# Two graph-attention layers on one core: layer-1 mask rows made by ScalarE inside the layer-0 attention, and layer-0 projection software-pipelined

## What is computed

```python
# layer 0, 8 heads of 64
data = (h @ W.T + b).reshape(N, 8, 64)
e = leaky_relu(src.T[:, :, None] + trg.T[:, None, :], 0.01) + adj     # src, trg: one number per node and head
x = x + softmax(e) @ data
# layer 1, 8 heads of 64, on h = relu(layernorm(x)) again
a = maximum(adj, eye)
atts = q @ k.T / 8 - 1e16 * (1 - a)
x = x + softmax(atts) @ v @ Wo
```

## Time and profile before

| | us |
|---|---|
| median of the runs | 4757.16 |
| the profiled execution | 4749.95 |
| its span | 4748.2 |
| PE busy in the span | 4406.2 (93%) |
| DVE busy | 3713.2 (78%) |
| POOL busy | 3452.3 (73%) |
| ACT busy | 3083.7 (65%) |
| layer-0 projection, first to last operation | 0 to 207 |
| layer-0 attention | 210 to 1688 |
| layer-1 projection | 1692 to 2017 |
| layer-1 attention | 2021 to 4748 |

### The profile page before, as it was taken

The page is one execution under the profiler, slowest core; times in us unless marked ns, Lnnn a source line. Parts: engine busy times, 40 slices in busy tenths (PEclk is TensorE's granted clock), DMA queues, the critical chain, the costliest instruction groups (busy, mean ns, idle before and its releaser), DMA issues. The chain is left out here.

```text
span 4748.2 us, 116365 instructions
## 1 busy us (share of the span) xinstructions
PE 4406.2 (93%) x42765; PEld 2133.6 (45%) x43276; DVE 3713.2 (78%) x7749; ACT 3083.7 (65%) x5769; POOL 3452.3 (73%) x2969
## 2 busy tenths in 40 slices
PE   6699999999999969859999999999999999999998
PEld 3222222222222224416556556555565565565554
DVE  4399999998999833377877968878878778688787
ACT  3355555555555523328878778778878787788785
POOL 2376676676677610029989889889989898899896
PEclk9899999999999979969999999999999999999999
DMA  3254454455453223362433533433434335334334
GB/s 136 67 163 136 130 158 143 136 149 155 136 144 114 73 99 114 105 202 82 143 102 104 152 107 98 146 94 113 143 90 130 114 98 157 101 95 151 98 110 127
DMA packets 424960, 583.35 MB, mean 123 GB/s; under 512 B 45584, under 2 KB 234384, under 8 KB 419408
## 3 DMA queue, kind: packets, MB, share of 16 engines
q1 hardware_dynamic: 419152, 559.08, 38.9%
q0 software_dynamic: 5120, 16.78, 1.2%
q10 hardware_dynamic: 128, 0.13, 0.0%
HBM read 499.02 MB, written 76.82 MB: 121 GB/s over the span
## 5 line engine op out<-in xcount | busy, mean ns | idle before, releaser
L1328 POOL TENSOR_TENSOR d_PL<-d_PF,d_PH 128x512 f16<-128x512 f32 x2048 | 2353.2, 1185 | 424.2 <-ACT d_PH L1373 420.3
L1430 DVE CUSTOM_DVE_ANT_0 d_junk<-d_gd,d_MR 128x512 bf16<-128x512 f32 x2112 | 1428.9, 686 | 380.7 <-issue 352.8
L1369 ACT ACTIVATE d_PF<-d_sc 128x512 f32<-128x512 f32 x2048 | 1279.7, 625 | 581.3 <-DVE d_sc L1517 378.4
L1373 ACT ACTIVATE d_PH<-d_sc 128x512 f16<-128x512 f32 x2048 | 1289.4, 630 | 0.0
L747 DVE SCALAR_TENSOR_TENSOR b_P<-b_R,u,b_A 128x512 f32<-128x512 f32 x1792 | 1195.6, 739 | 91.7 <-ACT b_A L650 48.9
L791 PE MATMUL b_acc<-b_P,V 128*64 128x512 f32 x4096 | 950.4, 601 | 47.8 <-DVE b_P L747 29.3
L1559 PE MATMUL d_gd<-d_KA,d_QA 128*128 128x512 f16 x2112 | 816.9, 387 | 129.0 <-DVE d_gm L1430 77.9
L1575 PE MATMUL d_sc<-d_QA,d_KA 128*128 128x512 f16 x2048 | 777.4, 380 | 20.1 <-ACT d_PH L1373 15.9
L1576 PE MATMUL d_sc<-d_QL,d_KB 128*128 128x512 f16 x2048 | 776.6, 379 | 0.0
L1596 PE MATMUL d_acc<-d_V,d_PH 128*128 128x65 f16 x8192 | 638.8, 192 | 3.5 <-ACT d_oC L1351 1.3
L1598 PE MATMUL d_acc<-d_V,d_PH 128*128 128x64 f16 x8192 | 639.9, 193 | 0.0
(11 more groups left out here) (132 smaller groups left out, 4225.7 us busy)
## 6 DMA issues: line engine op xcount, KB each, us to landing
d_stage<-in_adj SPq DMA_DIRECT2D x288, 256.0 KB, 3.4
d_V<-scratch_v SPq DMA_DIRECT2D x131, 520.0 KB, 4.4
b_stage<-in_adjT SPq DMA_DIRECT2D x128, 512.0 KB, 4.9
b_rows<-in_adj SPq DMA_DIRECT2D x112, 512.0 KB, 3.7
d_MT<-scratch_mt SPq DMA_DIRECT2D x35, 1024.0 KB, 6.4
d_KA<-scratch_kh SPq DMA_DIRECT2D x272, 128.0 KB, 2.9
d_KA<-scratch_kl SPq DMA_DIRECT2D x272, 128.0 KB, 3.2
d_KB<-scratch_kh SPq DMA_DIRECT2D x264, 128.0 KB, 3.2
```

The source lines that it names most:

```text
L1328: eng.tensor_tensor(PL[:, t % H_RING, :], PF[:, t % F_RING, :], PH[:, t % H_RING, :], ALU.subtract).then_inc(s_lowp if by_pool(t) else s_l ...
L1369: nc.scalar.activation(PF[:, t % F_RING, :], sc[(nb * TILES + t) % BANKS][:, :], ACT.Exp, scale=EXP_SCALE)
L1373: nc.scalar.activation(PH[:, t % H_RING, :], sc[(nb * TILES + t) % BANKS][:, :], ACT.Exp, scale=EXP_SCALE).then_inc(s_P, 1)
L1430: nc.vector.tensor_tensor_reduce(out=junk[:, gi % 2, :], in0=gd[gi % 2][:, :], in1=MR[:, s, c * QB:(c + 1) * QB], scale=1.0, scalar=-3.0e3 ...
```

## The change

The mask rows of layer 1 (`mr`, a new 4096 x 4096 bf16 array in DRAM) are made in layer 0's attention. Per block of 512 rows SP loads 16 chunks of 128 x 1024 of `adj` (`sign_rows`), ACT takes the sign of chunk minus limit and multiplies it by a constant, in two operations (`sign_row`), and SP stores the result (`store_rows`). This is at every odd step, after the sign of the transposed tile and, at step 1, ahead of the copies of the accumulators. Layer 1 loads `MR` in 4 rows of tiles of 1 MB per block (`load_mr`), and DVE keeps only the diagonal blocks (`mask_diagonal`). The ring of `adjT` stages goes from four to three. All loops of layer 0 are written out. The projection transposes group g+1 between the values of group g, with two buffers of `hT` and statistics two groups ahead, takes the first row maxima in 8 chunks of 128 x 2048, one per group, and loads the attention's first `R`, `am` and three stages itself.

```diff
 def layer0_project
-        rows = [sb(f"a_rows{s}", [P, N]) for s in range(SUB)]
-        hT = sb("a_hT", [P, 2, KC, QB], F16)
+        rows = sb("a_rows", [P, ROW_RING, CW])          # CW = N // 2, ROW_RING = 2
+        hT = sb("a_hT", [P, 2, 2, KC, QB], F16)
 SP
+            sp.dma_start(xg[:, :, :], DR["x"][0:QB, :]...).then_inc(s_x0, 16)
             (identf, wT, wn, pj, bcol, bias)
+            for ci in range(CHUNKS):                    # 8
+                if ci >= ROW_RING:
+                    sp.wait_ge(s_rank, ci - ROW_RING + 1)
+                (load rows[:, ci % ROW_RING, :])
+            (load T["stage"] 0, 1, 2)
+            sp.wait_ge(s_amax, 1)
             (store amax)
+            sp.wait_ge(s_rout, 16)
+            (load T["R"][:, 0], 8 broadcasts)
             sp.wait_ge(s_amout, 16)
+            (load T["am"][:, 0])
 POOL
+            load_x(1); load_x(2)
             for g in range(NB):
                 pool.wait_ge(s_wv, g * 4 + 4)
                 for s in range(SUB):
+                    if s == 2 and g + 3 < NB:
+                        load_x(g + 3)
                     weigh_v(g, s)
 DVE, per group
                 store_v(g, 0); clamp_t(g); store_v(g, 1)
+                hT_low(g + 1)
+                statistics(g + 2); norm(g + 2)
                 store_v(g, 2)
+                rank_chunk(g)
                 store_v(g, 3)
 ACT, per group: st, r, u, w, heads, then hT_high(g + 1), root(g + 2), relu(g + 2)
 PE, per group: stp, values 0, tq, values 1, turn(g + 1), values 2, values 3
 def layer0_attention
-    STAGES = 4
+    STAGES = 3
-            with eng.Fori(0, NB // 2 - 1) as i:
+            for nb in range(NB):
+            def sign_rows(nb, j):
+                if nb * CHUNKS + j:
+                    sp.wait_ge(s_ms, 2 * (nb * CHUNKS + j) - 1)
+                sp.dma_start(srow[:, :], src).then_inc(s_srow, 16)
+            def store_rows(nb, j):
+                sp.wait_ge(s_ms, 2 * (nb * CHUNKS + j + 1))
+                sp.dma_start(to, mrow[:, :]).then_inc(s_mr, 16)
 SP, per k, right after load_a(nb, k)
+                    if nb * CHUNKS + k >= SIGN_LAG:     # 2
+                        sign_rows(*divmod(nb * CHUNKS + k - SIGN_LAG, CHUNKS))
+                    if nb * CHUNKS + k > SIGN_LAG:
+                        store_rows(*divmod(nb * CHUNKS + k - SIGN_LAG - 1, CHUNKS))
 ACT
+            def sign_row(nb, par, j):
+                if j == 0:
+                    act.wait_ge(s_lim, nb + 1)
+                if nb or j:
+                    act.wait_ge(s_mr, 16 * (nb * CHUNKS + j))
+                act.wait_ge(s_srow, 16 * (nb * CHUNKS + j + 1))
+                nc.scalar.activation(mrow, srow, ACT.Sign, bias=nlim[:, par, s:s + 1]).then_inc(s_ms, 1)
+                act.wait_ge(s_ms, 2 * (nb * CHUNKS + j) + 1)
+                nc.scalar.activation(mrow, mrow, ACT.Copy, scale=-MASK_FLOOR).then_inc(s_ms, 1)
                     if m + SIGN_AHEAD < NT:
                         sign(nb, m + SIGN_AHEAD, first)
+                    if m % 2:
+                        sign_row(nb, par, m // 2)
...
                     if m == COPY_STEP and not first:
                         (copy_acc of 5 banks)
 DVE, at m == 0
+                        nc.vector.tensor_scalar(nlim[:, par, :], T["amax"][...], 1.0, -1.0, ALU.max, ALU.mult)
 def layer1_attention
-    CHUNK_STEPS = [FIRST_C + 5 * ci // 4 for ci in range(CHUNKS)]
+    ROW_FREE = (the step after the last guard of row s, in pair 2)      # steps 73, 80, 87, 93
+    ROW_SET = [free + 4 for free in ROW_FREE]
 SP
-                load_chunk(sp, ...)                     # 32 per block, DR["adj"], 256 KB
+                        for s in range(SUB):
+                            if step == ROW_FREE[s]:
+                                sp.wait_ge(s_gm, (nb * HP + HP - 1) * GUARDS + 2 * MC * (s + 1))
+                                load_mr(sp, (nb + 1) % NB, s)
 DVE
-                        for ci in range(CHUNKS):
-                            if step == CHUNK_STEPS[ci]:
-                                mask_chunk(nb + 1, (nb + 1) % NB, ci)
+                        for s in range(SUB):
+                            if step == ROW_SET[s]:
+                                mask_diagonal(nb + 1, (nb + 1) % NB, s)
 DVE, ahead of the first block
-            for ci in range(CHUNKS):
-                mask_chunk(0, 0, ci)                    # with two guards after each from the ninth on
+            for s in range(SUB):
+                mask_diagonal(0, 0, s)
+            for gi in range(GUARDS):
+                guard(0, gi, ...)
```

More of the change, by code:

```diff
@@ L244, in body @@
+            dve.wait_ge(s_wh, 2)
+            nc.vector.scalar_tensor_tensor(out=wpjS[:, 1, :, :], in0=wpj[:, :, :], scalar=W_SCALE, in1=wpjS[:, 0, :, :],
+                                           op0=ALU.mult, op1=ALU.subtract).then_inc(s_ws, 1)
+            statistics(1)
+            norm(1)
+            for g in range(NB):
                 store_v(g, 0)
+                clamp_t(g)
                 store_v(g, 1)
-                clamp_t(g)
-                rank(g, 1)
-                if not last:
-                    norm(g + 1)
+                if g + 1 < NB:
+                    hT_low(g + 1)
+                if g + 2 < NB:
+                    statistics(g + 2)
+                    norm(g + 2)
@@ L301, in body, with turn @@
                     nc.scalar.activation(heads[:, :, :, x, D + x], by_x[:, :, :, x], ACT.Exp, scale=0.99).then_inc(s_wv, 1)
-                if not last:
-                    root(g + 1)
-                    relu(g + 1)
-            in_blocks(act, body)
-            act.wait_ge(s_rout, 16 * NB + 16)
+                if g + 1 < NB:
+                    hT_high(g + 1)
+                if g + 2 < NB:
+                    root(g + 2)
+                    relu(g + 2)
+            act.wait_ge(s_rout, 16 * NB)
         @block.tensor
         def _(pe):
-            pe.wait_ge(s_w, 16 * 6)
+            def turn(g):
+                pe.wait_ge(s_h, g * SUB + SUB)
+                for c in range(KC):
+                    if g or c >= 2:
+                        pe.wait_ge(s_hT, g * KC + (c - 1))
+                    for s in range(SUB):
+                        mm = nc.tensor.transpose(tp[c % 2][:, s * P:(s + 1) * P], h[:, s, c * P:(c + 1) * P],
+                                                 T["identf"][:, :])
+                    mm.then_inc(s_tp, 1)
+            pe.wait_ge(s_id, 16)
+            turn(0)
+            pe.wait_ge(s_w, 16 * 5)
             for c in range(KC):
@@ L357, in body @@
                         mm.then_inc(s_tq, 1)
-            in_blocks(pe, body)
+                    if s == 1 and g + 1 < NB:
+                        turn(g + 1)
 def layer0_attention(nc, T, DR):
@@ L379, in layer0_attention @@
     AMAX_LOAD = 15
+    SIGN_LAG = 2
     TURN_STEPS = (3, 5, 7, 9, 11)
@@ L1323, in _ @@
                 sp.wait_ge(s_MT[i], 16 * (NB + (1 if i < GROUPS - 1 else 0)))
+            for s in range(SUB):
+                sp.wait_ge(s_MR[s], 16 * (NB + 1))
         def split(eng, engine, nb, t):
```

358 lines of the change are left out of this document (175 added, 183 removed).

## The result

The changed kernel takes 4775.77 us (median of 5 runs, 4774.46 to 4780.88) against 4754.87 of the kernel before in the same job: a ratio of 1.0046, 95% interval 1.0031 to 1.006. It is 21 us slower, where 4670 was forecast. The profiled executions stand 30.6 us apart (span 4778.8 against 4748.2), so the steps are accounted in that.

What follows compares the result with a forecast made beforehand. No engine full in the projection, PE bounds layer 0's attention, POOL layer 1's. Terms -50 + 15 - 5 + 21 - 12 - 56 = -87 from 4749.95 give 4663; the median 7.2 above, 4670 us; range 4625 to 4728.

Steps and rivals of the forecast that it cites:

- Projection and seam, -50: Start to layer 0's first attention product: shorter projection period and hidden loads bring it from 232.35 to 182, gain 50 us.
- ScalarE's pair at the block starts, +15: Layer 0's attention: sign and copy ahead of the accumulator copies lengthen PE's wait, 7 boundaries x 2.1 us, +15 us.
- Back edges, -5: Layer 0's attention: written-out loop removes three back edges with their longer PE waits, -5 us (0 to -6).
- Row chunks late, +21: Layer 0's attention: chunks for the maxima, issued later by SP, make DVE and PE wait, 3 us x 7 blocks, +21 us.
- the turns at 4 and 6: SP's turns whose chunks come late: k = 4 behind R's broadcasts (+1 us), k = 6 behind four diagonal loads (+1.6).
- Rival C: Layer 0's attention: SP's chain makes the tight row chunks wait in every block, slower; 3 us a chunk gives 4817; chance 0.08.
- Layer 1, -12 and -56: Layer 1: lead-in without its 32 chunks, -12 us; attention blocks without 256 DVE chunks, -56 us (-40 to -70).
- Rival A: Layer 1's attention: mask rows were free, DVE's chunks only filled spare time, so the 56 fall away: 4726; chance 0.10.

Runs made afterwards that it cites:

- e_act: Changed kernel keeping ScalarE's sign and copy on one chunk loaded once, without the mask rows' loads, stores and SP's waits; no whole time, layer-0 attention window 1458.7 us.
- e_none: Changed kernel without any mask-row loads, sign and copy, or stores in layer 0's attention; no whole time, attention window 1442.4 us against 1578.0.
- e_spread: Changed kernel with R's eight broadcasts issued one a turn (k = 3 to 10) and nothing else moved; 4730.35 us, ratio 0.9944 to the kernel before.
- e_actq_best: Changed kernel with mask rows issued by ScalarE, row chunks a turn earlier, R spread, accumulator copies before the pair, R before the maxima at the seam; 4615.75 us.
- e_actq: Changed kernel with the mask rows' loads and stores issued by ScalarE itself instead of SP; 4684.70 us, ratio 0.9849 to the kernel before.
- e_traffic: Changed kernel with mask-row loads and stores kept in SP's order, but without ScalarE's pair and SP's waits for it; 4685.46 us, ratio 0.9849 to the kernel before.
- e_seam: Changed kernel with R's eight broadcasts asked for before SP waits for the row maxima at the projection's end; 4776.14 us, ratio 1.0042 to the kernel before.

## Why the prediction was wrong

**Projection and seam, -50: -41.** First scores came at 26.87 (27 forecast), the maxima were ready at 160.01 (162.5). What failed is small: `am` was forecast to be asked for at 172, "behind the 2 MB of `R`", but SP took 15.51 us to issue `R`, longer than the 9.3 us of the store of `amax` that the sum used, so it went out at 176.17 and POOL had it ten later, where 4 to 5 were forecast.

**ScalarE's pair at the block starts, +15.** The size of the pair was right (1.13 and 1.06 us, 2.2 together) and so was the wait it gives (3.85 us in *e_act*, 4.0 forecast). The estimate of 2.3 us by the figure in the Trainium skill's page "ScalarE: Activation LUTs", section "Rules for kernel authors", was close too. The price was not right: behind the wait PE's 16 matmuls take some 2 us more (5.60 in the mean, 3.65 in *e_none*). Starts (27.0 - 12.1 = 14.9) and matmuls (7 x 1.95 = 13.6) make 28.5. That *e_act* lost only 16.3, next to the 15 forecast, is luck: fewer chunks were late there (10.4 us instead of 32.1). In the changed kernel the waits are 5.3 to 6.7 us, 40.4 in all.

**Back edges, -5.** Right: the starts of *e_none* are 12.1 instead of 16.8, though the edges were two and not three (waits of 3.75 and 3.67 us). The page "Runtime: NRT & Kernel Launch" of the Trainium skill, section "Instruction fetch mechanics", by which a taken branch out of the fetched pages stalls an engine, agrees with it in sign.

**Row chunks late, +21: this step failed.** The prediction wrote down the chain itself (`exp`, sign, copy, two stores, load, landing), and then counted it as time for one chunk at a time: issued 6.5 us after `exp`, landing 3.7 later, 8 chunks just in time, so only the turns at 4 and 6 were charged. Three things were missing. The landing was that of the kernel before (3.7; it became 6.5, and 5.3 in *e_none* already, where no mask row is moved: two steps later the chunk presumably goes out beside other loads). `R`'s eight broadcasts were charged 1 us a block, and cost 45 in all (*e_spread*). And a late chunk makes DVE late and a late DVE makes ScalarE and SP late, so that the next turn starts behind; this is how I read the 71.8 us that neither the pair nor the transfers cost alone. Measured, chunk waits rose by 100.7 us, the starts by 23.6, and the slower matmuls behind them add 7 x 2.1 = 15, less 1.9 for the one start that had them before: 137 against the 135.2 to be explained. That this is so close is partly luck, for the sum takes every wait of DVE as one of PE, as the prediction did ("each wait is PE's"). It isn't: *e_actq_best* has none of the 32.1 us of chunk waits of *e_none*, with the same 12.1 at the starts, and its window is only 17.3 us shorter.

**Rival C was what happened.** It named the place, the chain and the point ("a landing of about 6.5 us in place of 3.7"), and the landing was 6.5. It got 0.08, on the ground that the DMA engines are below half busy. They were in the kernel before (0.44 in the window) and are 0.61 busy in the changed one. But *e_actq* has them 0.65 busy and is 91 us faster: the order in the queue was the limit, not the engines. Its mechanism was right, though its 3 us a chunk for 56 chunks was too much (49 waits of 2.5 us). Its reading of the landing as the cause wasn't right: in *e_actq* and *e_traffic* landings were as long and the kernels 90 us faster.

**Layer 1, -12 and -56: -9.6 and -53.4.** Right, mechanism and size; pairs 2 and 3 end 77 to 79 us apart, the first scores come 77 us after the first DMA issue (75 forecast). Rival A falls. POOL's mean operation fell by 15 ns, 31 us of the 53 over 2048; where the other 22 come from no run shows. The section "SBUF: two separate sides" of the Trainium skill's page "SBUF — State Buffer", by which such a DVE operation and POOL lock each other out for a whole instruction, fits that.

What stays open: which wait of the late chain swallows the seam's 11 us, whether the loss would come with four stages too, and whether a second buffer for the mask rows would do what a queue of their own does (no run has one).

## What to carry to other kernels

Before you add a DMA that waits for a computing engine to a queue, list what stands behind it there, with the time at which each is needed: a wait is paid by all that follows, and it feeds back where the engine that is made late is the one the queue waits for. When a queue is shared, change the order or the owner first; here the same bytes and the same arithmetic span 4806 to 4616 us by their order and their queue alone. And price a stall of TensorE by the step after it too: here 3.85 us of waiting cost 5.8 (*e_act*).

## What the runs showed of the hardware

- The price of a wait of PE is not its length alone. Behind waits of 1.72 to 1.91 us the next 16 matmuls take 3.65 to 3.76 us, with the granted clock at 1.00 (1.00 is 2.4 GHz). Behind 3.85 us (*e_act*) they take 5.10 to 6.56 us and behind 4.8 us 5.00 to 6.49, with the granted clock at 0.50 (1.2 GHz) for 4 us at some of these starts, as from 743 to 747 us in *e_act*. The kernel before has two long waits at its back edges and pays this at one of them: 5.54 us behind 3.75 (the earlier trace rows shows the first 8 of the 16), with the clock at 0.71 from 776 to 780 us, but 3.76 us behind 3.67, with the clock at 1.00 throughout.

```profile
777.16 5.54 PE L791 MATMUL b_acc<-b_P,V 128*64 128x512 f32 x16 [3.75 <-ACT b_oT L683]
...
1137.77 3.76 PE L791 MATMUL b_acc<-b_P,V 128*64 128x512 f32 x16 [3.67 <-ACT b_oT L683]
```

- What eight broadcasts of 256 KB cost SP depends on what it issued around them. They hold it for 8.1 to 9.6 us in the blocks of the changed kernel, for 6.0 to 6.8 us in *e_actq*, where SP issues no mask rows, and for 15.51 us at the seam of the changed kernel, right behind the 2 KB store of `amax` and with the DMA engines only 0.40 busy. Ahead of that store, in *e_seam*, the same eight take 4.23 us, although a row chunk and three stages had just been asked for and the DMA engines were 0.96 busy:

```profile
133.61 4.23 SPq L153 DMA_DIRECT2D R<-scratch_r  x8
```

- Spread one a turn, the broadcasts land in a median of 5.3 to 6.5 us; in the other versions of the changed kernel it is 9.5 to 10.4.
- A DMA issued by ScalarE costs it little. Each takes 0.33 us to issue in *e_actq*, its copies behind the pair stand 0.5 us idle for the pair's result and that issue, and in *e_actq_best* the blocks are 177.9 us apart, less than the 180.3 before.
